# GpSimd waits for the rotation loop's first pass before it scatters the records of two edge sorts

## The reference, cut to what matters

```python
def step(mat, t):
    i, j, theta = t                  # src, dst, edge_weight
    ri, rj = mat[i], mat[j]
    mat = mat.at[i].set(cos(theta) * ri - sin(theta) * rj)
    mat = mat.at[j].set(sin(theta) * ri + cos(theta) * rj)
```

## Time and profile before

| | us |
|---|---|
| time, median of 3 runs | 7296.96 (7293.32 to 7312.87) |
| span of the profiled execution | 9062.1 |
| engines busy in it: PE, DVE, ACT, POOL | 4683.8, 5139.2, 1224.9, 4305.5 |

### The profile page before, as it was taken

How to read it: one execution, slowest core, us unless ns; L and a number is a source line. 1 busy time by engine, 2 the same in 40 slices (tenths; PEclk the granted TensorE clock), 3 DMA queues, 4 the chain that set the end, 5 groups by cost and what they waited for, 6 DMA issues and landing times. The chain is left out here.

```text
span 9062.1 us, 179398 instructions
## 1 busy us (share of the span) xinstructions
PE 4683.8 (52%) x60555; PEld 3816.1 (42%) x60555; DVE 5139.2 (57%) x12108; ACT 1224.9 (14%) x2828; POOL 4305.5 (48%) x3974
## 2 busy tenths in 40 slices
PE   0000000488732555476766767766676777445552
PEld 0000000366621444356666556666566665323331
DVE  7996000377754444655665455555455555557767
ACT  0000000122201111111111011111011111122220
POOL 5887777200063555135655055554255552066640
PEclk9999999999955555689999889898889988755555
DMA  0000000000012333155552255551355540133320
GB/s 24 3 1 1 1 1 1 1 0 0 4 26 65 101 101 101 48 167 156 158 157 62 88 147 161 152 150 31 117 154 158 156 120 21 30 94 98 98 75 24
DMA packets 708570, 691.60 MB, mean 76 GB/s; under 512 B 234981, under 2 KB 589355, under 8 KB 708165
## 3 DMA queue, kind: packets, MB, share of 16 engines
q0 software_dynamic: 227328, 446.06, 18.1%
q1 hardware_dynamic: 480846, 240.51, 9.6%
HBM read 766.03 MB, written 77.58 MB: 93 GB/s over the span
## 5 line engine op out<-in xcount | busy, mean ns | idle before, releaser
L1669 POOL DMA_INDIRECT kvring<-kvtab,oth x1776 | 1834.4, 1033 | 1619.5 <-PE ea_psg L1731 923.2
L1069 POOL DMA_INDIRECT e_hg<-htab,oth_d x992 | 991.8, 1000 | 1130.9 <-issue 713.4
L1720 PE MATMUL ea_pss<-ea_qb,ea_kT 128*128 128x128 f32 x7104 | 1198.0, 306 | 0.0
L1720 PEld LDWEIGHTS ea_pss<-ea_qb,ea_kT 128*128 128x128 f32 x7104 | 1113.8, 224 | 32.3
L1790 DVE TENSOR_TENSOR acc<-ea_psg,acc 128x64 f32 x1776 | 399.0, 225 | 1161.3 <-remote 1049.8
L1731 PE MATMUL ea_psg<-ea_mix,kvring 128*64 128x64 f32 x14208 | 581.9, 240 | 887.6 <-DVE ea_mix L1832 877.2
L1731 PEld LDWEIGHTS ea_psg<-ea_mix,kvring 128*64 128x64 f32 x14208 | 522.1, 152 | 984.8 <-issue 691.2
L255 POOL DMA_INDIRECT sb_rec<-srawrec,splacei x392 | 430.9, 1099 | 960.5 <-PEq L56 815.9
L1196 PE MATMUL e_psg<-e_Em,e_hg 128*32 128x32 f32 x15872 | 569.9, 245 | 439.6 <-issue 399.4
L1764 ACT ACTIVATE ea_kT<-ea_pst 128x512 f32<-128x512 f32 x888 | 481.9, 595 | 2201.5 <-remote 1331.3
L1196 PEld LDWEIGHTS e_psg<-e_Em,e_hg 128*32 128x32 f32 x15872 | 439.2, 146 | 622.0 <-issue 524.2
(11 more groups left out here) (506 smaller groups left out, 8250.9 us busy)
## 6 DMA issues: line engine op xcount, KB each, us to landing
ea_qb<-qtab SPq DMA_DIRECT2D x1776, 64.0 KB
qtab<-at_qst SPq DMA_DIRECT2D x75, 512.0 KB, 3.3
kvring<-kvtab,oth POOLq DMA_INDIRECT x1776
e_stack<-ohtab SPq DMA_DIRECT2D x744, 32.0 KB
kvtab<-at_kvst SPq DMA_DIRECT2D x75, 256.0 KB, 2.7
e_hg<-htab,oth_d POOLq DMA_INDIRECT x992
ea_mk<-mtab SPq DMA_DIRECT2D x444, 3.0 KB
htab<-Hd SPq DMA_DIRECT2D x2, 3200.0 KB, 11.6
```

The lines of the kernel that those rows point to most:

```text
L1069: pool.indirect_dma_start(out=hg[:, b % RING, u, :], out_offset=None, in_=htab, in_offset=bass.IndirectOffsetOnAxis(ap=oth[:, b * 4 + u:b ...
L1669: pool.indirect_dma_start(out=kv[:, b % R, u, :], out_offset=None, in_=kvtab, in_offset=bass.IndirectOffsetOnAxis(ap=oth[:, b * QB + u:b * ...
L1720: mm = pe.matmul(ps_s[r % 2][:, u, k * 2 * HN:(k + 1) * 2 * HN], kT[:, r % 2, u, k, :], qb[:, r, u, :], start=False, stop=True, skip_group ...
```

## The change

GpSimd, which has just raised `listed`, waits for `rs` to reach 3 and only then goes on to the scatters of the two sorts.

```diff
                 scatter(pool, steps, B["placei"], B["rec"], sc[0:2], P * RT - 1)
                 pool.sem_inc(s["listed"], 1)
+                pool.wait_ge(s["rs"], 3)
                 for q, t, pair in zip(sorts, sems, (sc[2:4], sc[4:6])):
                     pool.wait_ge(t["padst"], 16)
                     pool.wait_ge(t["placed"], 1)
```

## The result

The change makes the kernel slower. The median is 7416.82 us after (7408.88 to 7423.95, 4 runs) against 7304.91 us before on the same chip (7293.32 to 7313.32, 4 runs: the three given above and a fourth): 111.9 us more, a ratio of 1.0157 with a 95% interval of 1.0145 to 1.0169. The prediction was 7406 us, 109 us more than the 7297 it started from.

The account below looks back on a forecast made before the run. It took GpSimd's scatter queue to end the rotation phase in both kernels: 87 scatters put off to 898 us cost 87 x 1.26 = 109 us, so 7297 + 109 = 7406 us, range 7287 to 7435.

Parts of the forecast that it names:

- The sign and the size: GpSimd's scatters before the rotation phase's end: slower by 109 us, 87 scatters put off at 1.26 us; slower given 70%.
- The slow first batch: Rotation loop's first batch, R at 1701 instead of about 873: the 828 us excess taken as mostly absent from timed runs.
- the books of the execution: Whole kernel: 1765 us of profile excess; edge stages can return 1229, so 536 must come from elsewhere.
- records being drained one by one: Loop's first batch: profiler records drained with semaphores behind them, about 1.3 to 1.4 us per instruction; argued, not shown.
- The release: GpSimd's new wait: rs is 3 at about 898 us (890 to 905), the first batch's R at 873.
- GpSimd ends the phase in both kernels: Rotation phase's end: GpSimd's scatters outlast the loop, ending at 1787 us before and 1896 after, so nothing covers the cost.
- the pace of a scatter beside the running loop: GpSimd beside the rotation loop: 1.6 us a scatter taken, with bounds of 1.26 and 1.86.
- near 1.33, where before is just covered by the loop: 118: GpSimd beside the rotation loop: the scatter pace at which the wait would cost most, 118 us.
- The loop's end: Rotation loop: 24.76 us a batch, last R at 1641 us, a phase that ends with the loop at 1656.
- The slow batch is real: Rival, 16%, faster: scatters hold up the loop's first pass; up to 587 us less, 6710 us.
- The loop hides GpSimd: Rival, 14%, same: the loop ends last in both kernels, with scatters under 1.14 us or batches slowed to 27.4; 7297 us.
- First-time code: Rotation loop's first pass: the second batch took 28.4 us against 24.76, so new code alone costs some 4 us.

Follow-up runs that it names:

- e1: The kernel before, unchanged, profiled once more: 7301.9 us, with a profiled span of 7300.1 us.
- e3: The changed kernel with GpSimd waiting for rs 9 (four passes, eight batches) instead of rs 3: 7554.41 us, ratio 1.0346 to before.
- e4: The changed kernel with GpSimd waiting for vs 1, a ScalarE signal ahead of the loop's body, instead of rs 3: 7358.35 us, ratio 1.0076 to before.
- e5: The changed kernel, wait kept, with 96 of 272 source-sort columns of this phase left unscattered: 7299.01 us, ratio 0.9983 to before.
- e2: The changed kernel with GpSimd waiting for one batch (rs 2) instead of rs 3: 7387.66 us, ratio 1.0120 to before.
- e6: The kernel before, without the wait, with 96 of 272 source-sort columns of this phase left unscattered: 7289.24 us, ratio 0.9972 to before.
- e8: The changed kernel with the rs 3 wait moved between the two sorts, ahead of the source sort's scatters: 7309.94 us, ratio 0.9997 to before.

## Why the prediction was right, and where it was not

**The sign and the size.** Both held: the 664 scatters wait for the third `rs`, only some 6 us of slack cover the delay at the end, and the cost is 112 us where 109 was forecast.

**The slow first batch.** The prediction set aside a stretch of 828 us in its only profile, because the delays went by the number of instructions and because the books of the execution did not close with it. e1 shows that this was right: R starts at 874.1 instead of 1701.0, 827 us earlier, in the same kernel. That the stretch belongs to that one execution is shown. That it comes from records being drained one by one is still only argued, and why one execution of the program was stretched and another not stays open.

**The release.** It was worked out as rs = 3 at 898 and the first R at 873; the first scatter starts at 895.9 and the first R at 870.5. The 18 us for the straight part ahead of the body stood in no row; in e1 VectorE ends it with its first sum into `T` at 844.9, 18.1 us behind its start at 826.9.

**The step that failed: "GpSimd ends the phase in both kernels".** Before, the loop ends it (e1: 1666.2, and the fetch at 1667.0). The term behind it is the pace of a scatter beside the running loop: 1.6 us was taken, "nearer to `type_counts`", and it is 1.33 (after) where the bounds were 1.26 and 1.86. That made GpSimd's end late by nearly the same in both kernels: 1787 and 1896 forecast, 1667.0 and 1779.2 measured, 120 and 117 too late, and the errors cancel in the difference. That they cancel to 3 us is luck. The sum with the measured pace is the one that the prediction had as its most: "near 1.33, where before is just covered by the loop: 118". With 6 us of slack off it, it is 112. So the forecast was near for a partly wrong reason. From 1.33 up to 1.86 its sum moves only from 118 to 102, and this part of its strength was no luck; below 1.33, where the loop ends the phase before, it falls to 79 at 1.26, and the kernel stands just at that edge. `type_counts` was the wrong neighbour although VectorE loops in both, and VectorE's busy share does not tell the two apart: 76% in the rotation loop (586 of 767 us) with 1.33 us a scatter, and 81% in e1's `type_counts` (113 of 140 us from 1719 to 1859 us, 88 scatters) with 1.6. What VectorE's work does to a scatter, beyond its share, is not shown.

**The loop's end.** 1656 was forecast for a phase that ends with the loop; in e1 it ends at 1667.0. The batch is (1647.8 - 870.5) / 31 = 25.1 us in after and the same in e1, not 24.76: 31 of them are 10 us more. The 24.76 came from batches that had no scatters beside them, and e3 shows that difference inside one run, 24.5 against 25.2.

**The rivals.** *The slow batch is real*: refuted by e1, and e4 prices the first pass beside scatters at a microsecond or two, where 240 would have been needed. *The loop hides GpSimd*: false for this kernel, true with 96 fewer scatters (e5), and before itself stands only 6 us on that side of the line. The prediction asked for a pace under 1.14 us in after, and it is 1.33, or for a batch slowed to 27.4 us, and it is 25.1.

**First-time code.** The prediction put some 4 us on new code, from a second batch of 28.4 us in the profile of before. In after the second R starts at 894.5, 24.0 us behind the first, and in the eight other profiles 23.2 to 25.8 us behind it. That is around the average batch of 25.1, and single batches of these profiles vary from 23.2 to 27.5. The 4 us are not seen again. The Trainium skill, Runtime: NRT & Kernel Launch, section Instruction fetch mechanics, says that a taken branch to a target outside the window of loaded pages forces a fetch before execution goes on, and the prediction read from it that a first pass fetches. The trace agrees that fetches lie there: in e1 q8 has 5 packets from 835 to 900 us and none in the rest of the loop. But no run here shows a microsecond that they cost the loop.

## What to carry to other kernels

Before a stretch of a profile is explained, its span has to be held against the timed runs: a profiled execution that is 24% too long can put its excess into a few stages, and a change aimed at those gains nothing. A wait ahead of a long queue of small operations costs what the queue has no slack for: find the end of that engine's queue and the end of the phase in one trace, subtract what lies between, and count each microsecond of waiting beyond that as nearly one, less where the operations put off would have been slow ones (0.96 here beside the loop, 0.82 beside the sort and up to the loop). And an engine that does 1.3 us operations one by one for 900 us should start them when their inputs are ready, even if another engine is slowed a little meanwhile: holding them back until the first pass was over brought the first R some 3 us forward (870.5 against 874.1), and cost 112. The loop's own end shows no clear gain: the last copy of M starts at 1660.9 to 1667.6 in after and e2 to e5, with the wait, and at 1663.7 to 1670.1 in e1 and e6 to e8.

## What the runs showed of the hardware

Two profiled executions of one kernel differ by 1762 us in span (9062.1 and 7300.1). In the long one a semaphore behind a burst is seen late in proportion to the burst (41.9 us for 32 instructions of TensorE, 89.2 for 64) and in the short one after 1.2 us.

With VectorE busy for 76% of the loop, GpSimd's scatters slow only from 1.26 to 1.33 us start to start; the median one lasts 0.96 us there as it does alone. In `type_counts`, with VectorE at 81%, they are 1.6 us apart. Beside the scatters a batch of the loop takes 25.2 us, without them 24.5 (e3).

TensorE's granted clock in after is 0.95 of full speed while the loop runs (895 to 1662 us) and 0.50, the lower of the two levels, 1.2 GHz, in the 118 us in which TensorE stands still while GpSimd finishes. The next phase has it low in e1 too, where the gap is missing:

```profile
1667.00:1790.00 123.00, 51.64 (x245) 29.58 (x245) 89.98 (x174) 0.00 (x0) 89.45 (x74) 0.50 0.20 39
```

Nor does standing still go with the low clock each time: in e1 it is 1.00 from 757 to 800 us, ahead of the loop, with no matmul in the stretch. So the idle stretch costs its own length and no row shows a further cost through the clock, which agrees with a difference in the whole time (111.9 us) close to the difference in the phase's end (112.1).
